# Gated cross attention with a feed-forward part: 16-bit projections, and the attention result of both batches of a group at once

## What is computed

```python
x = x + tanh(g_xattn[0]) * xattn(layernorm(x), ctx, Wq, Wk, Wv, Wo)
x = x + tanh(g_ffn[0])   * ffn(layernorm(x), ternary(W1), b1, ternary(W2), b2)
# xattn: q = x @ Wq, k = ctx @ Wk, v = ctx @ Wv (ctx: 128 x 192), 16 heads of 16 numbers,
#        softmax(q k^T * 0.25) v for each head, then @ Wo
# ffn:   gelu(x @ W1^T + b1) @ W2^T + b2, hidden width 1024, weights of -1, 0, 1
```

## Time and profile before

| | |
|---|---|
| median of the runs shown | 1665.97 us (2 runs, 1662.24 and 1669.7) |
| the profiled execution | 1664.17 us, its span 1662.4 us |
| granted clock of PE, mean | 0.984 |
| busy share of the span | PE 91%, DVE 90%, PE's weight loads 61%, ACT 57%, POOL 40% |
| the chain that ended last | PE 55%, DVE 26%, issue 13%, ACT 3% |

### The profile page before, as it was taken

How to read it: one execution, slowest core, us unless ns; L and a number is a source line. 1 busy time by engine, 2 the same in 40 slices (tenths; PEclk the granted TensorE clock), 3 DMA queues, 4 the chain that set the end, 5 groups by cost and what they waited for, 6 DMA issues and landing times.

```text
span 1662.4 us, 48262 instructions
## 1 busy us (share of the span) xinstructions
PE 1508.0 (91%) x14501; PEld 1007.7 (61%) x14501; DVE 1489.1 (90%) x4379; ACT 939.8 (57%) x1799; POOL 668.8 (40%) x813
## 2 busy tenths in 40 slices
PE   3899999999999999999999999987999999999998
PEld 2566666666666666666666666655666666666665
DVE  7799999999999999999999999987888888888886
ACT  2456666665656666565656566654555555555554
POOL 5354555455555545554555545552111111111111
PEclk9899999999999999999999999996999999999999
DMA  2333333333333333333333333321010110101101
GB/s 78 92 99 85 96 84 88 93 86 97 84 96 83 97 84 94 86 87 95 86 97 83 98 83 95 81 49 55 26 38 25 38 38 25 38 25 38 38 25 51
DMA packets 207471, 117.93 MB, mean 71 GB/s; under 512 B 24912, under 2 KB 207184, under 8 KB 207440
## 3 DMA queue, kind: packets, MB, share of 16 engines
q1 hardware_dynamic: 207440, 117.54, 26.2%
HBM read 32.53 MB, written 16.78 MB: 30 GB/s over the span
## 4 chain that ended last, share of the span: by engine, by line
PE 55%; DVE 26%; issue 13%; ACT 3%; DVEq 2%; ACTq 0%; DMA 0%
PE bank L1069 12%; PE bank L312 9%; PE bank L1098 5%; PE bank L1099 5%; DVE smax L751 5%; PE bank L336 5%; PE bank L319 4%; PE bank L303 4%; DVE rstd L691 3%; DVE xres L796 3%; DVE k L721 3%; PE bank L392 2%; DVE rstd L693 2%; DVE y L1056 2%; DVE rstd L684 2%
## 5 line engine op out<-in xcount | busy, mean ns | idle before, releaser
L924 POOL TENSOR_TENSOR probl<-prob 128x512 f16<-128x512 f32 x512 | 529.2, 1042 | 531.2 <-ACT prob L602 530.3
L602 ACT ACTIVATE prob<-bank,masks 128x512 f32<-128x512 f32 x512 | 345.4, 688 | 138.9 <-PE bank L371 138.9
L751 DVE TENSOR_REDUCE smax<-bank 128x4 f32<-128x512 f32 x512 | 348.2, 681 | 13.5 <-PE bank L336 9.7
L1085 DVE TENSOR_TENSOR hidl<-hid 128x512 f16<-128x512 f32 x256 | 226.0, 883 | 80.5 <-ACT hid L1080 79.7
L1080 ACT ACTIVATE hid<-bank,b_sb 128x512 f32<-128x512 f32 x256 | 176.1, 688 | 211.3 <-PE bank L1069 205.3
L1069 PE MATMUL bank<-y,w1T 128*128 128x512 f16 x1024 | 264.6, 381 | 29.2 <-DVE y L1056 28.0
L1163 POOL TENSOR_TENSOR xres<-xres,b2g 128x1024 f32 (+1 forms) x32 | 75.7, 2366 | 431.4 <-ACT yln L1033 413.5
L1098 PE MATMUL bank<-w2T,hid 128*128 128x256 f16 x1024 | 237.4, 273 | 0.6 <-ACT w2T L1013 0.6
L1099 PE MATMUL bank<-w2T,hidl 128*128 128x256 f16 x1024 | 237.4, 273 | 0.0
L336 PE MATMUL bank<-k_rows,q_rows 64*128 64x128 f16 x2048 | 226.8, 220 | 5.6 <-DMA q_rows<-smaxT 3.4
L371 PE MATMUL bank<-q_rows,k_rows 64*128 64x128 f16 x2048 | 201.7, 219 | 0.8 <-DMA q_rows<-smaxT 0.8
(11 more groups left out here) (92 smaller groups left out, 2555.7 us busy)
## 6 DMA issues: line engine op xcount, KB each, us to landing
q_rows<-q SPq DMA_DIRECT2D x512, 64.0 KB, 2.5
k_rows<-k SPq DMA_DIRECT2D x512, 64.0 KB, 2.5
xres<-in_x_dram SPq DMA_DIRECT2D x64, 256.0 KB, 2.7
out_dram<-ystage SPq DMA_DIRECT2D x32, 512.0 KB, 2.9
ctx_sb<-in_ctx_dram SPq DMA_DIRECT2D x64, 192.0 KB, 3.2
q_rows<-smaxT SPq DMA_DIRECT2D x128, 8.0 KB
w_raw<-in_L_ffn_W_dram SPq DMA_DIRECT2D x2, 1024.0 KB, 7.0
prob<-in_L_xattn_Wq_dram SPq DMA_DIRECT2D x1, 256.0 KB, 4.2
```

The costliest lines, as they stand in the source:

```text
L602: act.activation(prob[u][:], st_bank[u % 2][:], ACT.Exp, bias=0.0, scale=masks[g.parity][:, 2 + b:3 + b]).then_inc(exp_done, 1)
L751: dve.tensor_reduce(smax[:, b, u * UH:(u + 1) * UH], sm_bank[u % 2][:].rearrange("p (h j) -> p h j", h=UH), AX.X, ALU.max).then_inc(max_ta ...
L924: pool.tensor_tensor(probl[u][:], prob[u][:], prob[u][:].bitcast(BF16)[:, 1::2], ALU.subtract).then_inc(prob_split, 1)
```

## The change

- Every 32-bit operand of a projection becomes a pair of 16-bit numbers, high and low. x, the context and the exponentials are split by POOL in their own place (`low_x`, `low_ctx`, `low_prob`: the low part overwrites the lower half of each number); the weights are split once at the start, by ACT and DVE. A projection is then three 16-bit matmuls (high x high, high x low, low x high) for one 32-bit matmul before. X and C are eight 16-bit transposes each, and their copy is one ACT copy of 1024 16-bit columns.
- V's halves are added in PSUM: W is three matmuls of 32 columns for a head (before, two of 48), and each batch has one value bank. DVE then has one reciprocal (`sum_weighed`) and one multiply (`normalise`) for a batch. A, O and `add_attention` treat both batches of a group at once, one group late.
- `low_q` and `low_k` are one instruction each (before, two), with a scale. q and k move by five DMAs for a batch (before, eight); x is loaded 512 KB at a time.
- Mean and variance are taken for four batches at a time, on DVE in every second group (`seed_x`), and the Newton steps of the root are on POOL (`root_x`).
- The order on every engine is written anew.

The diff, cut to its core ("left" is how many groups come after this one):

```diff
-                last = pe.matmul(pj_bank[:, m * T:(m + 1) * T], wq_sb[:, k, m * P:(m + 1) * P],
-                                 xlnT[:, k, :], start=(k == 0), stop=(k == KD - 1))
+                for i, (wp, xp) in enumerate(SPLIT):
+                    last = pe.matmul(by_batch(m), wq16[:, wp, k, m * P:(m + 1) * P],
+                                     typed(xT16[:, xp, k, :], xp).rearrange("p (b s) -> p b s", b=2),
+                                     start=(k == 0 and i == 0 and m == 0), stop=(k == KD - 1 and i == 2),
+                                     skip_group_check=True)
...
+                v_low = v16_all[g.parity][:, first:first + VC]
+                v_high = v16_all[g.parity][:, first + VH:first + VH + VC]
                 high = prob[u][:].bitcast(BF16)[:, 2 * c * S + 1:2 * (c + 1) * S:2]
-                pe.matmul(o, high, v, start=True, stop=False)
-                last = pe.matmul(o, probl[u][:, c * S:(c + 1) * S], v, start=False, stop=True)
+                low = prob[u][:].bitcast(F16)[:, 2 * c * S:2 * (c + 1) * S:2]
+                pe.matmul(o, high, v_high, start=True, stop=False)
+                pe.matmul(o, high, v_low, start=False, stop=False)
+                last = pe.matmul(o, low, v_high, start=False, stop=True)
...
+            tr = transpose_max(pe, g, 1, tr)
             if left >= 2:
-                pe.wait_ge(v_split, g.n + 1)
-                project_q(pe, g2, 0)
+                project_q(pe, g2, 1)
                 tr = transpose_ctx(pe, g2, tr)
-                project_q(pe, g2, 1)
...
+            scores(pe, g, 1, 1, (g1, 1, 0) if left >= 1 else None)
             weigh(pe, g, 0, 3)
+            if left >= 1:
+                tr = transpose_max(pe, g1, 0, tr)
+                if left >= 2:
+                    pe.wait_ge(k_split, g.n + 3)
+                project_v(pe, g1, 0)
+            scores(pe, g, 1, 2, (g1, 1, 1) if left >= 1 else None)
+            weigh(pe, g, 1, 0)
+            if left >= 1:
+                project_v(pe, g1, 1)
             if left >= 3:
                 tr = transpose_x(pe, g.after(3), tr)
...
+            scores(pe, g, 1, 3, (g1, 1, 2) if left >= 1 else None)
...
             weigh(pe, g, 1, 1)
-            tr = transpose_attn(pe, g.batch(0), 0, tr)
-            if left >= 1:
-                project_v(pe, g1, 1)
+            if not first:
+                tr = project_out(pe, before, tr)
...
+            exponentials(act, g, 1, 2)
+            if left >= 1:
+                high_v(act, g1)
             if left >= 3:
                 copy_xT(act, g3)
-            exponentials(act, g, 1, 2)
...
+            act.activation(halves_of(g, QH), pj_halves, ACT.Identity, bias=0.0,
+                           scale=1.0 / WS).then_inc(q_high, 1)
...
+        def seed_x(dve, half, i):
...
+            if i == 0:
+                dve.wait_ge(x_in, 16 * (half + 1))
+                for b in range(QB):
+                    last = dve.bn_stats(stats[:, b, :], row_of(half * QB + b))
...
+        def low_x(pool, g):
+            pool.wait_ge(ln_done, 2 * (g.n + 1))
+            x = xln[:].rearrange("p b d -> p (b d)")
+            pool.tensor_tensor(x.bitcast(F16)[:, 0::2], x, x.bitcast(BF16)[:, 1::2], ALU.subtract).then_inc(x_split, 1)
...
+            dve.scalar_tensor_tensor(halves_of(g, QL), pj_halves, 1.0 / WS,
+                                     halves_of(g, QH), ALU.mult,
+                                     ALU.subtract).then_inc(q_split, 1)
...
+            dve.tensor_tensor(attn[b][:], pv[:, :, 0:HD], rsum[:, b, :].unsqueeze(2).to_broadcast([P, HEADS, HD]),
...
+                if g.parity == 1 and left >= 6 and i < SEED_PARTS:
+                    seed_x(dve, g.half + 3, i)
...
             round_max(dve, g, 1)
-            norm(10)
+            norm(0)
+            norm(1)
...
             low_max(dve, g, 1)
+            norm(2)
+            if left >= 1:
+                take_max(dve, g1, 0, 0)
+            norm(3)
             if left >= 2:
                 low_q(dve, g2)
...
+                sum_weighed(dve, before, 1)
+                norm(5)
+                normalise(dve, before, 1)
...
+                low_attn(dve, before)
+            if left >= 2:
+                low_k(dve, g2)
...
-            pool.tensor_tensor(probl[u][:], prob[u][:], prob[u][:].bitcast(BF16)[:, 1::2],
+            pool.tensor_tensor(prob[u][:].bitcast(F16)[:, 0::2], prob[u][:], prob[u][:].bitcast(BF16)[:, 1::2],
...
+            if left >= 2:
+                move_k(sp, g.after(2), 0, split2)
+            if g.parity == 0 and left >= 6:
+                sp.wait_ge(ln_ready, x_past)
+                load_x(sp, g.half + 3)
```

More of the change, by code:

```diff
@@ L798, in dve_first, with add_attention @@
+        def add_attention(dve, g):
+            dve.wait_ge(projected, g.n + 1)
+            if isinstance(g.half, int) and g.n == 0:
+                dve.wait_ge(gate_scaled, 1)
+            rows = xres[:, bass.ds(g.batch(0), 2), :]
+            dve.scalar_tensor_tensor(rows, tr_bank[:].rearrange("p (b d) -> p b d", b=2), gate_xw, rows, ALU.mult,
+                                     ALU.add).then_inc(x1_done, 1)
         def dve_first(dve):
+            dve.memset(vone[:], WS)
+            dve.memset(smax16_all[:], -MAX_UNIT)
```

702 lines of the change are left out of this document (397 added, 305 removed).

## The result

The changed kernel takes 1797.59 us (median; 1794.09 to 1801.1) against 1665.97 us before: ratio 1.080, 95% interval 1.074 to 1.086. It is 8% slower. The forecast was 1666 us with a range of 1540 to 1725 us, so the time lies 132 us above the forecast and outside the range.

The account below looks back on a forecast made before the run. The prediction took the sequence of PE's pieces and their handing over to DVE and ACT as the bound, not busy shares. 1664 - 84 (groups) + 78 (statistics) + 6 (start) = 1664 us, 1666 at the median; range 1540 to 1725 us.

Parts of the forecast that it names:

- The walk: One group's sequence over PE, ACT and DVE in seven pieces: 15.65 us against 16.96 us, -84 us over 64 groups.
- piece f: high_k and low_k before V may start: 1.85 us, with PE standing for 1.0 us.
- splits it (0.4): DVE's splitting of the reduced maximum beside PE's S, W and half Q, ahead of M: 0.4 us.
- piece c: S, W, half Q, S, W beside DVE's addition and maximum, then M and the other half of Q: 2.82 us.
- The stalls: PE idle thrice a group: O behind copy of X (about 1 us), A behind multiply (1.2), V behind low_k (1).
- Even 15.7, odd 18.4 us: Sign expected in the profile after: even groups 15.7 us, odd groups 18.4 us, M waiting on the maximum's second part.
- The statistics, +78 us: Odd groups: statistics, copy and aggregations ahead of low_max, 2.3 us, plus 0.4 us waiting for x, in 29 groups.
- W at 0.32 us: Each W on PE, twelve matmuls of 32 columns, priced at 0.32 us from 0.24 to 0.32 us.
- The start, +6 us: POOL's larger clears, low_x and twelve weight pieces before the first Q: 0 to 12 us later, taken as 6.
- The moves at nothing: K's last four moves go out some 5.5 us before their rough scores: no cost; if late, up to 0.5 us a group.
- Rival 3: Slower: the 512 KB load of x lands late and holds up M and PE; 1700 to 1735 us, chance 0.13.
- Rival 1 and 2: First: engine loads decide, about 14 us a group, 1485 us, chance 0.17. Second: statistics are covered, 1586 us, chance 0.15.

Follow-up runs that it names:

- e3: Changed kernel with round_max and low_max as tensor_reduce copies, the 1/64 moved to ACT's copy, low half of the maximum left out as zero: 1671.9 us, ratio 1.0043.
- e12: Changed kernel with POOL's low_prob as two instructions of 256 columns in place of one of 512, DVE untouched: 1775.9 us, ratio 1.0651.
- e5: Changed kernel with the reciprocal and multiply of the batch before placed ahead of low_q and one take_max on DVE: 1736.0 us, ratio 1.0446.
- e6: Changed kernel with ACT's copy of X ahead of high_v: 1784.8 us, ratio 1.0723.
- e1: Changed kernel with the statistics of x in odd groups behind low_max, not ahead of it: 1779.9 us, ratio 1.0686.
- e14: Kernel of e10 with all four statistics steps in the even group ahead of low_v: 1543.6 us, ratio 0.9261.
- e2: Changed kernel with useless PE matmuls: 17 ahead of the wait for low_max in odd groups, 7 meant ahead of the wait before V: 1767.0 us, ratio 1.0614.
- e13: Kernel of e3 with PE filled as in e2: 1686.8 us, ratio 1.0115.
- e4: Changed kernel with eight row transfers a batch again in place of five: 1817.4 us, ratio 1.0917.
- e10: Changed kernel, take_max writing the 16-bit maximum (low half zero), bn_stats in even groups, x loaded earlier, multiply, copy of X and low_attn moved ahead: 1562.4 us, ratio 0.9376.

## Why the prediction was wrong

The walk was right nearly everywhere, and two of its seven pieces were not. The even group from 622.41 to 639.73 in the trace after, the one of e3 from 603.14 to 618.76, and what the prediction gave:

| piece | predicted | after | e3 |
|---|---|---|---|
| g, V | 1.97 | 2.06 | 2.06 |
| a, X until O starts | 2.15 | 2.15 | 2.15 |
| b and c, O until the second half of Q is through | 4.14 | 4.86 | 4.25 |
| d, until A starts | 2.98 | 3.05 | 3.04 |
| e, A and K | 2.56 | 2.54 | 2.54 |
| f, until V starts | 1.85 | 2.66 | 1.58 |
| sum | 15.65 | 17.32 | 15.62 |

The match of the sums, 15.65 and 15.62 us, is in part luck: piece f was taken 0.27 us too long, and c, d and g together 0.26 us too short.

**The step that failed is "splits it (0.4)" in piece c, and piece f, where nothing of DVE was counted ahead of `low_k`.** `round_max` and `low_max` were taken at what they cost before, 0.18 us each. The prediction had itself read a tiny copy on DVE at 0.17 us "where POOL is nearly idle and 0.56 us as now" and counted it for the copy alone. The change shifts both steps of the maximum from beside POOL's mask steps to beside `low_prob` and `low_x`, and there each waits for the rest of a 1.04 us instruction: 0.60 and 0.71 us on the mean. That `low_max` stands ahead of `low_attn` and `low_k` in one queue then carries 0.8 us into piece f, beside 0.7 us in piece c. Removing the cause removes 126 of the 132 us (e3), and e3's 1671.9 us lie 6 us from the forecast of 1666.

That it is POOL's running instruction, and not the layout or the engine's load, rests on three things: the durations by what POOL runs beside them, each ending 0.03 us after POOL's, e3 (another instruction for the same copy, no wait), and e12 (an instruction half as long, a wait half as long). The Trainium skill states it (SBUF — State Buffer, section "Who interferes with whom"): a DVE instruction in a 2-port mode, which `tensor_scalar` can enter, and a GpSimd instruction block each other, and so do a DVE instruction with two SBUF inputs and a GpSimd instruction that reads SBUF, the later one until the first has ended; `tensor_reduce` on trn2 never does. By that rule the trace agrees: 0.60 us for the `tensor_scalar` and 0.71 us for the `scalar_tensor_tensor`, 0.17 us for the `tensor_reduce`. In which mode the `tensor_scalar` ran, no trace here shows.

Point by point:

- **The stalls.** O behind the copy of X about 1 us, A behind the multiply 1.2 us, V behind `low_k` 1 us: in the even group after they are 0.81, 0.97 and 1.53 us (1.16 of it in front of M). Right in place, and e5 comes near A's full price (62 of 70 us). What each is worth is another matter: O's is covered in groups at the lower clock (e6).
- **Even 15.7, odd 18.4 us.** Close once the two steps don't wait (15.62 and 18.52 in e3), wrong in the changed kernel (17.89 and 20.25).
- **The statistics, +78 us.** The odd groups of e3 are longer by 2.9 us, predicted 2.7, but of other parts:

```profile
628.89 0.29 PE L395 MATMUL bank<-ident,smax 128*128 128x128 f16 x1 [2.31 <-DVE smax L911]
628.97 1.49 PE L341 MATMUL bank<-xT,wq 128*128 128x256 bf16 x6
```

  M waits 2.31 us, 0.71 us of it because x hasn't landed, so the statistics are 1.6 us (predicted 2.3) and x 0.7 us (predicted 0.4). The half of Q behind M then runs at the lower clock, 0.6 us longer than at 610.94 in the even group, and that term the prediction didn't have. The three errors cancel, which is luck. And the price isn't that of M alone: moved behind `low_max` they gain 18 us and not 55 (e1), because `low_q` and A stand behind them. Only in the gap ahead of `low_v` do they cost nothing (e14).
- **The clock.** No step of the prediction had it. Filling gains 31 us in the changed kernel (e2), with its own cost some 45 us by the estimate above; in e3 no run prices it (e13). In good part it is a consequence: with the two waits gone and nothing changed on PE, e3 has 0.953 in place of 0.900, and with all orders it is 0.988.
- **W at 0.32 us.** Right: twelve matmuls from 609.91 to 610.23 in PE's timeline. The floor of about 25 ns from start to start that the Trainium skill states (TensorE: Matmul & The Clock Gate, section "Wait — 56ns, not 53.3ns?") holds here, at 26 to 27 ns for 32 columns.
- **The start, +6 us.** The fifth `low_k` starts at 102.66 us in e3 and at 97.58 us before: 5 us. About right; the first groups differ in length too, so the start alone isn't measured.
- **The moves at nothing.** Right for the five moves: PE's weight loads wait 0.2 us in all for q and k rows in the changed kernel (60 to 1250 us), though the transfers of 128 KB land 4.0 us after the issue. What the merging gained, 20 us by e4, the prediction didn't count.
- **Rival 3, the load of x.** It sets in only where DVE is early enough to ask: 4.9 us in all in the changed kernel, 24.6 us in e3. As the slower case it was the wrong mechanism.
- **Rival 1 and 2.** The loads don't decide the changed kernel, since orders alone change its time. But e14, with no statistics on the path and full clock, takes 15.0 us a group, of which PE stands for 1.7 us; PE's own work is then 13.3 us, not the 12.4 us of the prediction's sum. Over 0.9, as rival 1 reckons, 13.3 us is 14.8 us: with PE's work rightly summed, that rival gives about what the best order reached. Its own arithmetic was off a little as well (16.96 less 14 is 2.96, not 2.8).

## What to carry to other kernels

When a change moves small DVE instructions, lay both timelines over each other and ask what POOL runs beside them in the new order: here a `tensor_scalar` or `scalar_tensor_tensor` from SBUF on 16 numbers cost up to a whole instruction of POOL (1.01 us in place of 0.17), and it costs it in front of everything that is queued behind it. Two cures were measured: use a form that isn't held up (`tensor_reduce` in e3), or write the result in the instruction that reads PSUM anyway (e10, which leaves out the low half of the maximum as e3 does). And where the chain of waits names a transfer, compare the start of the instruction with the end of its other sources before believing it: here 0.33 us after a matmul's slot told more than the name. And before filling an engine's idle time, see on which side of its wait the filling will stand.

## What the runs showed that was not expected

- `low_k`, with one operand in PSUM and one in SBUF, isn't held up: in 29 of 59 groups it begins under a long instruction of POOL, and it takes 0.67 us there as in the others. Nor are the bn_stats, with one SBUF operand: 84 of them begin under one and take 0.41 us, as they do alone. One SBUF operand isn't enough to be safe, though: the copy of the statistics has one too, and takes 0.69 us in e14.
- The same filling gains 31 us in the changed kernel and loses 15 us in e3, and 14 us of either is its own cost, because seven of its matmuls stand behind a wait and not in it.
- A wait on a semaphore that a running transfer also raises is put down to that transfer, 26 us in 51 groups after the change, although `high_q` began 0.17 us after the end of Q's last matmul with or without that name.
